# Own weights and reciprocals through a scratch in device memory, the maxima's copy on VectorE, and the reciprocals' rows behind the second stack pair

## The chip, the cores and the metric

The kernel runs on one core of a Trainium2 chip. The metric is the device time of that core in microseconds (us), from launch to end. Engines: TensorE (PE, its weight loads PEld), VectorE (DVE), ScalarE (ACT), GpSimd (POOL) and SyncE (SP), which here only issues DMAs. Each engine runs its own instructions in order and waits on semaphores that the others and the DMAs raise.

## The reference

Eight batches of 512 rows of width 512. A layer of cross attention with 16 heads of width 32 is added to x, and then a two-layer network of hidden width 2048, whose last 128 output columns come from one of eight experts per batch. Each query also attends to itself by one extra score, the "own" score.

```python
query = seq2 + b_self
key = jnp.concatenate([seq1 + b_prev, seq2 + b_self], 1)
value = jnp.concatenate([seq1, seq2], 1)
q, k, v = ...                                   # 16 heads of 32
score_prev = jnp.einsum('bhqd,bhkd->bhqk', q, k[:, :, :l1]) * SCALE
score_self = (q * k[:, :, l1:]).sum(-1, keepdims=True) * SCALE
score_prev = jnp.where(mask[:, None, None, :], score_prev, -jnp.inf)
weights = jax.nn.softmax(jnp.concatenate([score_prev, score_self], -1), axis=-1)
attn = jnp.einsum('bhqk,bhkd->bhqd', weights[..., :-1], v[:, :, :l1])
attn = attn + weights[..., -1:] * v[:, :, l1:]
x = x + (attn.transpose(0, 2, 1, 3).reshape(b, l2, H * DH) @ Wo + bo)
h = jax.nn.gelu(x @ W1 + b1, approximate=False)
x = x + jnp.concatenate([h @ W2 + b2, h @ We[indices] + be[indices]], axis=-1)
```

## The kernel before

**Stages.** First the attention of all eight batches (to about 1220 us of the span), then the output projection and the network, batch by batch. Matmuls are split into high and low parts, three matmuls per product. In attention a batch is four *groups* g of four heads each; group number G = 4 b + g. A group is 16 *tiles* i (four key blocks t times four heads j). The batches 1 to 6 are one hardware loop on every engine, batch 0 and batch 7 are unrolled. The order on each engine is written out by hand, by tables of places (g, i).

**A group on PE** (`batch` in the tensor block): per tile i one score matmul of group G (`score_tile`), the maximum matmuls of group G + 1 (`max_tile`), and thirds of the projections of group G + 2; in g = 0 also the value projections. At i = 11 come the denominators of group G - 1 (`denominators`), the own scores of G + 1 and the transpose of its maxima (`own_scores`, `turn_max`). After the last tile `value_run` multiplies the probabilities by the values.

**Around it.** ACT makes the probabilities p_f from the scores (`probabilities`), POOL adds them to p_sum (`add_probabilities`), DVE reduces the maximum tiles to m_col (`maximum`). The maximum matmuls of G + 1 read *stacks*, which SP copies from `parts` by DMA in two pairs of heads (`stack_pair(..., 0)` and `(..., 1)`, three DMAs per head, and a mask row in g = 2 and 3). The second pair may only be written once score tiles 14 and 15 of the present group have run. `m_col` holds four maxima per query block; `maxima_twice` doubles them to eight columns on ACT at i = 12, then `turn_max` turns them. DVE then takes the maximum with the own scores (`own_max`), splits it (`m_parts`) and SP and ACT copy it into the stacks (`maxima`). ACT turns the own scores into own weights in `own_s` (`own_weight`, i = 15).

**The two spreads.** `own_s` and `den` are 128 x 128 tiles in SBUF: row 32 t + j belongs to query block t and head j, and only 4 rows of each 32 mean anything. POOL needs the own weights (`own_value`) and DVE the reciprocals of the denominators (`normalize`) with each head's row repeated on 32 partitions: `own_rows` and `over_den_rows`, the two halves of the tile `spread`. SP makes each by four DMAs, one per query block t, whose source is four partitions, each read 32 times:

```python
def rows_of(tile, t):
    return bass.AP(tile[:, :].tensor, DH * t * P, [[P, HG], [0, DH], [1, P]])
```

**SP's order in a group**: in g = 0 and 1 the 16 input loads of the next batch (`load`, 64 KB each), which DVE turns at (0, 9) to (1, 15) (`turn`); the first stack pair of G + 2; `maxima` of G + 1; the reciprocals' rows of G - 1 (`over_den`); the second stack pair of G + 2; the own weights of G + 1 (`own_weights`); the store of the numerators of G - 2 (`store`). In batch 7 weight pieces for the second stage take the place of the loads (`wide`, `wide_late`), with `attended` and `residual` for its first batch.

## Time and profile before

| | us |
|---|---|
| median of 3 runs (2031.56 to 2033.59) | 2032.14 |
| the profiled execution | 2025.96 |
| its span, first to last instruction | 2024.1 |
| PE busy | 1760.7 (87%) |
| DVE, ACT, POOL busy | 839.9, 705.0, 651.8 |
| mean granted TensorE clock | 0.925 |
| shares of the chain that ended last: PE, SP's queue, DMAs, DVE, ACT | 72%, 18%, 5%, 2%, 1% |

The profiled execution took 1.9 us more than its span, and 6.2 us less than the median of the runs. Busy shares are means over two unlike stages: in the second one PE is busy all the time. So the page is read by stretches, a group of the attention at a time. A group ends where `value_run` (L1435) ends. Line numbers are those of the kernel before; a "hole" is time in which PE sits idle, and the row says what ended it.

### The profile page before, as it was taken

The numbers are of one execution on the slowest core, as the hardware profiler recorded it, in microseconds if no ns is written. First come the engines' busy times: TensorE is split into PE (matmuls) and PEld (weight loads), VectorE is DVE, ScalarE is ACT, GpSimd is POOL, SyncE is SP. The second block draws the span as 40 slices with busy tenths as digits, with TensorE's granted clock in tenths as the row PEclk, the third lists the DMA queues.
The fourth block names the chain that finished last, engine by engine and source line by source line (L and its number), as shares of the span: only waits on it lengthen the run. The fifth ranks groups of instructions, "written<-read, shape, count | busy, mean of one in ns | idle before, by whom it ended". The sixth has DMA issues, their size and how long they took to land.

```text
span 2024.1 us, 29434 instructions
## 1 busy us (share of the span) xinstructions
PE 1760.7 (87%) x9024; PEld 1335.4 (66%) x9024; DVE 839.9 (41%) x1338; ACT 705.0 (35%) x1255; POOL 651.8 (32%) x518
## 2 busy tenths in 40 slices
PE   6989879888788878788799546999999999999998
PEld 5656556556556556466566224888888888888886
DVE  4554454454544554454454623432323232323222
ACT  3344333334333433343344323432323232323231
POOL 2356356464563654645553422010101010101010
PEclk8989889989899889889799668999999999999999
DMA  6443443443534434444433343332313131413121
GB/s 136 75 82 71 86 85 78 78 86 75 94 81 77 87 70 91 80 82 75 85 75 74 95 88 104 107 61 68 74 51 78 47 78 47 83 44 81 46 42 21
DMA packets 379888, 153.69 MB, mean 76 GB/s; under 512 B 287571, under 2 KB 339795, under 8 KB 379811
## 3 DMA queue, kind: packets, MB, share of 16 engines
q1 hardware_dynamic: 374966, 152.05, 36.4%
q10 hardware_dynamic: 4844, 0.78, 0.2%
q8 instruction: 28, 0.46, 0.1%
q14 instruction: 50, 0.40, 0.1%
HBM read 60.97 MB, written 24.15 MB: 42 GB/s over the span
## 4 chain that ended last, share of the span: by engine, by line
PE 72%; SPq 18%; DMA 5%; issue 3%; DVE 2%; ACT 1%; DVEq 0%; POOL 0%; ACTq 0%
PE ps_proj L1354 14%; PE ps_max L1306 6%; PE ps_max L1308 6%; PE ps_max L1307 6%; SPq L390 5%; PE ps_score L1422 5%; PE ps_num L1435 5%; SPq L409 5%; PE ps_max L1395 4%; SPq L373 4%; PE ps_num L1306 3%; PE ps_num L1308 3%; PE ps_num L1307 3%; PE ps_score L1306 3%; PE ps_score L1308 3%; PE ps_score L1307 3%
## 5 line engine op out<-in xcount | busy, mean ns | idle before, releaser
L1016 DVE TENSOR_REDUCE m_col<-ps_max 128x1 f32<-128x512 f32 x512 | 335.5, 686 | 398.7 <-PE ps_max L1395 396.5
L794 ACT ACTIVATE p_f<-ps_score 128x512 f32<-128x512 f32 x512 | 302.6, 598 | 443.2 <-PE ps_score L1422 389.2
L670 POOL TENSOR_TENSOR p_sum<-p_sum,p_f 128x512 f32<-128x512 f32 x256 | 326.1, 1305 | 0.2 <-ACT p_f L794 0.2
L1395 PE MATMUL ps_max<-stacks 97*128 97x512 f32 x512 | 197.8, 438 | 86.9 <-DMA stacks<-parts 80.8
L1354 PE MATMUL ps_proj<-in_hi,w_hi 128*128 128x512 f32 x512 | 223.1, 436 | 48.3 <-DVE parts L998 36.0
L1209 DVE TENSOR_TENSOR h_lo<-h_f,h_hi 128x512 fp32r<-128x512 f32 x128 | 88.0, 688 | 414.2 <-ACT h_hi L898 414.0
L1422 PE MATMUL ps_score<-stacks 99*128 99x512 f32 x512 | 229.6, 450 | 29.5 <-ACT p_f L794 28.0
L712 POOL TENSOR_TENSOR z_f<-z_f,a_raw 128x512 f32<-128x512 f32 x28 | 35.8, 1290 | 676.9 <-ACT z_f L907 654.4
L1354 PE MATMUL ps_proj<-in_lo,w_hi 128*128 128x512 f32 x512 | 221.3, 432 | 0.0
L1354 PE MATMUL ps_proj<-in_hi,w_lo 128*128 128x512 f32 x512 | 217.7, 425 | 0.0
L667 POOL TENSOR_TENSOR p_sum<-p_f 128x512 f32<-128x512 f32 x128 | 168.0, 1334 | 71.3 <-PE ps_max L1449 71.3
L1395 PEld LDWEIGHTS ps_max<-stacks 97*128 97x128 f32 x512 | 105.4, 210 | 120.3 <-issue 78.6
L658 POOL TENSOR_TENSOR v<-v,spread 128x512 f32<-128x512 f32 x32 | 41.5, 1298 | 411.4 <-DMA spread<-own_s 411.4
L1422 PEld LDWEIGHTS ps_score<-stacks 99*128 99x128 f32 x512 | 106.2, 208 | 97.9 <-ACT p_f L794 41.9
L1354 PEld LDWEIGHTS ps_proj<-in_hi,w_hi 128*128 128x128 f32 x512 | 109.2, 213 | 77.3 <-DVE parts L998 39.6
L1354 PEld LDWEIGHTS ps_proj<-in_lo,w_hi 128*128 128x128 f32 x512 | 109.9, 215 | 26.6
L1354 PEld LDWEIGHTS ps_proj<-in_hi,w_lo 128*128 128x128 f32 x512 | 106.9, 209 | 26.1
L1435 PE MATMUL ps_num<-p_f,v_st 128*32 128x512 f32 x1024 | 118.4, 603 | 4.5 <-DVE num L1047 4.2
L675 POOL TENSOR_TENSOR in_lo<-turned,in_hi 128x512 fp32r<-128x512 f32 x64 | 80.9, 1291 | 115.5 <-ACT in_hi L732 115.4
L1306 PE MATMUL ps_num<-y_hi,w_hi 128*128 128x512 f32 x256 | 101.7, 397 | 16.7 <-ACT h_hi L898 9.4
L1307 PE MATMUL ps_num<-y_lo,w_hi 128*128 128x512 f32 x256 | 101.3, 396 | 0.0
L1308 PE MATMUL ps_num<-y_hi,w_lo 128*128 128x512 f32 x256 | 101.3, 396 | 0.0
(141 smaller groups left out, 2987.5 us busy)
## 6 DMA issues: line engine op xcount, KB each, us to landing
stacks<-parts SPq DMA_DIRECT2D x384, 128.0 KB, 2.4
raw<-in_x_dram SPq DMA_DIRECT2D x128, 64.0 KB, 2.1
raw<-in_fside_BxSxS_dram SPq DMA_DIRECT2D x128, 64.0 KB, 2.2
spread<-own_s SPq DMA_DIRECT2D x128, 64.0 KB
spread<-den SPq DMA_DIRECT2D x128, 64.0 KB
attn_scratch<-num SPq DMA_DIRECT2D x32, 256.0 KB, 7.2
x_raw<-in_x_dram SPq DMA_DIRECT2D x128, 64.0 KB, 2.1
we_raw<-in_L_cond_We_dram SPq DMA_DIRECT2D x32, 256.0 KB, 2.9
```

The costliest lines, as they stand in the source:

```text
L390: sp.dma_start(f(stacks[DH * part:DH * (part + 1), r, j]), f(pair)).then_inc(stacked[r][j], DMA)
L667: pool.tensor_tensor(p_sum[:, j], p_f[:, place_of(0, j)], p_f[:, i], ALU.add).then_inc(sum_made, 1)
L670: pool.tensor_tensor(p_sum[:, j], p_sum[:, j], p_f[:, i], ALU.add).then_inc(sum_made, 1)
L794: act.activation(p_f[:, i], ps_score[i % 2][:, :], ACT.Exp, scale=SCALE).then_inc(p_made, 1)
L1016: dve.tensor_reduce(m_col[:, n % C, n // C:n // C + 1], ps_max[n % 3][:, :], AX.X, ALU.max).then_inc(max_made, 1)
L1306: pe.matmul(ps, left[0], right[0], start=first, stop=False)
L1307: pe.matmul(ps, left[0], right[1], start=False, stop=False)
L1308: return pe.matmul(ps, left[1], right[0], start=False, stop=last)
L1354: mm = pe.matmul(ps, left, right, start=(m == 0), stop=(m == 3 * C - 1))
L1395: pe.matmul(ps_max[n % 3][:, :], q_st[0:KM, r, j, P * t:P * (t + 1)], k_st[0:KM, r, j, :], start=True, stop=True).then_inc(max_mm, 1)
L1422: pe.matmul(ps_score[i % 2][:, :], k_st[0:KS, r, j, P * t:P * (t + 1)], q_st[0:KS, r, j, :], start=True, stop=True).then_inc(score_mm, 1)
L1435: mm = pe.matmul(ps_num[at, :], v_st[:, t, P * g + DH * j:P * g + DH * (j + 1)], p_f[:, i], start=(t == 0), stop=(t == C - 1))
```

## The change

Own weights: ACT waits for its own activation and stores the whole tile `own_s` to a scratch in device memory (`own_scratch`), right after the activation at i = 15; SP then reads it back by four DMAs, one per head j, each from four rows of 512 bytes (one per query block) repeated over 32 partitions. Reciprocals: the same through `den_scratch`; ACT stores `den` after the last probabilities tile of the group, and for the very last group SP does. `over_den` stands behind the second stack pair instead of ahead of it, and at the end of attention behind `w2_piece(3)`. The doubling of the maxima on ACT (16 columns) is gone; DVE copies them to 28 more columns at i = 10 (`maxima_rows`), and `turn_max` and `denominators` make 32 rows per block instead of 8, so that all 128 rows of the tiles are defined. `m_hi` is gone: both steps of `m_parts` write `m_neg`, and the wait for the previous maxima's DMAs stands ahead of the first.

```diff
-            def rows_of(tile, t):
-
-                return bass.AP(tile[:, :].tensor, DH * t * P, [[P, HG], [0, DH], [1, P]])
-
             def own_weights(b, c):
 
                 G = C * b + c
-                sp.wait_ge(ow_made, G + 1)
-                for t in range(C):
-                    sp.dma_start(own_rows[:, P * t:P * (t + 1)], rows_of(own_s[c % 2], t)).then_inc(ow_landed, DMA)
+                sp.wait_ge(ow_stored, DMA * (G + 1))
+                for j in range(HG):
+                    sp.dma_start(own_rows[DH * j:DH * (j + 1), :].rearrange("k (t q) -> k t q", t=C),
+                                 own_dram[c % 2, :, j].partition_broadcast(DH)).then_inc(ow_landed, DMA)
...
             def over_den(b, c):
 
-                G = C * b + c
-                sp.wait_ge(rden_made, G + 1)
-                for t in range(C):
-                    sp.dma_start(over_den_rows[:, P * t:P * (t + 1)], rows_of(den, t)).then_inc(over_den_landed, DMA)
+                sp.wait_ge(den_stored, DMA * (C * b + c + 1))
+                for j in range(HG):
+                    sp.dma_start(over_den_rows[DH * j:DH * (j + 1), :].rearrange("k (t q) -> k t q", t=C),
+                                 den_dram[:, j].partition_broadcast(DH)).then_inc(over_den_landed, DMA)
...
-                    if more:
-                        stack_pair(*after(b, g, 2), 1)
...
+            store_over_den()
+            w2_piece(3)
             over_den(B - 1, C - 1)
-            w2_piece(3)
...
-            def maxima_twice(b, c):
-
-                G = C * b + c
-                act.wait_ge(max_made, TILES * (G + 1))
-                act.copy(m_col[:, :, HG:2 * HG], m_col[:, :, 0:HG]).then_inc(m_twice, 1)
-
...
                 act.activation(own_s[c % 2][:, :], own_s[c % 2][:, :], ACT.Exp, scale=SCALE).then_inc(ow_made, 1)
+                wait(act, ow_landed, HG * DMA * (G - 1))
+                act.wait_ge(ow_made, G + 1)
+                act.dma_start(own_dram[c % 2].rearrange("t k q -> (t k) q"), own_s[c % 2][:, :]).then_inc(ow_stored, DMA)
+
+            def store_over_den(b, c):
+
+                G = C * b + c
+                act.wait_ge(rden_made, G + 1)
+                wait(act, over_den_landed, HG * DMA * G)
+                act.dma_start(den_dram.rearrange("t k q -> (t k) q"), den[:, :]).then_inc(den_stored, DMA)
...
+            def maxima_rows(b, c):
+
+                G = C * b + c
+                dve.wait_ge(max_made, TILES * (G + 1))
+                dve.tensor_copy(m_col[:, :, HG:DH].rearrange("p t (n j) -> p t n j", j=HG),
+                                m_col[:, :, 0:HG].unsqueeze(2).to_broadcast([P, C, DH // HG - 1, HG])).then_inc(m_rows, 1)
...
-                dve.tensor_scalar(m_hi[:, :], m_s, -1.0, None, ALU.mult).then_inc(m_hi_made, 1)
                 pb, pc = after(b, c, -1)
                 wait(dve, m_landed[pc % 2], C * DMA * (2 * pb + pc // 2 + 1))
+                dve.tensor_scalar(m_neg[:, :], m_s, -1.0, None, ALU.mult).then_inc(m_hi_made, 1)
...
-                    mm = pe.matmul(ps_max[0][DH * t:DH * t + 2 * HG, 0:P], m_col[:, t, :], f(ident[:, :]),
+                    mm = pe.matmul(ps_max[0][DH * t:DH * (t + 1), 0:P], m_col[:, t, :], f(ident[:, :]),
...
-                    one_at = ones[:, C - 1 - j:C - 1 - j + 2 * HG]
+                    one_at = ones[:, HG - 1 - j:HG - 1 - j + DH]
```

SP, group (0, 2) from its `maxima` to its `store`, before. `spread<-den` are the reciprocals' rows, `spread<-own_s` the own weights', `stacks<-parts` here the second stack pair with its mask row:

```order
L397 DMA stacks<-m_neg 2x4x128 [waits m_lo_made]
L397 DMA stacks<-m_neg 2x4x128
L416 DMA spread<-den 128x1x128 [waits rden_made]
L416 DMA spread<-den 128x1x128 x3
L384 DMA stacks<-mask_scratch 1x2x512 [waits score_mm]
L390 DMA stacks<-parts 32x1024 [waits score_mm]
L390 DMA stacks<-parts 32x2x512 x2
L409 DMA spread<-own_s 128x1x128 [waits ow_made]
L409 DMA spread<-own_s 128x1x128 x3
L420 DMA attn_scratch<-num 128x512 [waits attn_made]
```

The same place now:

```order
L399 DMA stacks<-m_neg 2x4x128 [waits m_lo_made]
L399 DMA stacks<-m_neg 2x4x128
L386 DMA stacks<-mask_scratch 1x2x512 [waits score_mm]
L392 DMA stacks<-parts 32x1024 [waits score_mm]
L392 DMA stacks<-parts 32x2x512 x2
L420 DMA spread<-den_scratch 32x4x128 [waits den_stored]
L420 DMA spread<-den_scratch 32x4x128 x3
L407 DMA spread<-own_scratch 32x4x128 [waits ow_stored]
L407 DMA spread<-own_scratch 32x4x128 x3
L425 DMA attn_scratch<-num 128x512 [waits attn_made]
```

The stack pair moved ahead of both spreads, these now stand side by side, their shape went from 128 x 1 x 128 to 32 x 4 x 128, and they wait for a DMA's landing instead of an engine.

ACT, group (0, 1) from i = 12 to its end, before:

```order
L766 COPY m_col<-m_col 128x4x4 [waits max_made]
L773 COPY own_s<-ps_max 128x128 [waits den_made,ow_landed,own_mm]
L794 ACTIVATE p_f<-ps_score 128x512 [waits sum_made,av_mm,score_mm] x2
L780 DMA stacks<-m_neg 2x4x128 [waits m_lo_made]
L780 DMA stacks<-m_neg 2x4x128
L794 ACTIVATE p_f<-ps_score 128x512 [waits sum_made,av_mm,score_mm]
L787 ACTIVATE own_s<-own_s 128x128 [waits ov_made,own_less_made]
L794 ACTIVATE p_f<-ps_score 128x512 [waits sum_made,av_mm,score_mm]
L732 CAST in_hi<-turned 128x512 [waits v2_mm,turn_made] x4
```

and now:

```order
L773 COPY own_s<-ps_max 128x128 [waits den_made,ow_stored,own_mm]
L804 ACTIVATE p_f<-ps_score 128x512 [waits sum_made,av_mm,score_mm] x2
L780 DMA stacks<-m_neg 2x4x128 [waits m_lo_made]
L780 DMA stacks<-m_neg 2x4x128
L804 ACTIVATE p_f<-ps_score 128x512 [waits sum_made,av_mm,score_mm]
L787 ACTIVATE own_s<-own_s 128x128 [waits ov_made,own_less_made]
L790 DMA own_scratch<-own_s 128x128 [waits ow_made,ow_landed]
L804 ACTIVATE p_f<-ps_score 128x512 [waits sum_made,av_mm,score_mm]
L797 DMA den_scratch<-den 128x128 [waits rden_made]
L738 CAST in_hi<-turned 128x512 [waits v2_mm,turn_made] x4
```

The copy of the maxima left ACT, and a store now stands on each side of the last probabilities tile.

## Rows read from the trace of the kernel before

**Rows 1.** Windows (length; busy of PE, PEld, DVE, ACT, POOL; PEclk, DMA share, GB/s).

```profile
812.00:848.70 36.70, 27.48 (x161) 18.75 (x161) 18.87 (x31) 15.96 (x31) 21.07 (x17) 0.86 0.49 92
848.70:881.60 32.90, 26.85 (x165) 18.95 (x162) 15.84 (x27) 12.00 (x23) 19.73 (x17) 0.90 0.38 74
881.60:913.20 31.60, 27.32 (x161) 18.82 (x162) 16.18 (x27) 12.00 (x23) 17.44 (x15) 0.89 0.38 76
...
194.10:1055.30 861.20, 711.15 (x4133) 503.23 (x4129) 420.79 (x696) 325.27 (x624) 457.22 (x361) 0.90 0.43 81
...
1090.70:1220.00 129.30, 75.61 (x401) 44.51 (x400) 57.32 (x80) 42.21 (x81) 52.65 (x41) 0.72 0.39 85
...
1055.30:1090.70 35.40, 35.35 (x213) 26.09 (x209) 16.27 (x27) 14.16 (x27) 19.27 (x16) 1.00 0.35 69
...
595.00:623.00 28.00, 24.07 (x160) 16.66 (x158) 15.84 (x27) 12.03 (x23) 13.29 (x12) 1.00 0.41 83
...
102.90:194.10 91.20, 79.81 (x485) 56.12 (x481) 49.65 (x84) 40.41 (x77) 49.50 (x40) 0.91 0.43 81
```

**Rows 2.** Waits, whole span (engine, line, releaser: total us, times, longest).

```profile
PE ps_max L1395 <- DMA stacks<-parts: 80.8, 21, 6.0
...
DVE turned L990 <- DMA raw<-in_fside_BxSxS_dram: 49.3, 10, 7.8
...
PE ps_max L1412 <- ACT m_col L766: 48.0, 9, 7.2
...
PE ps_proj L1354 <- DVE parts L998: 36.0, 6, 7.5
```

**Rows 3.** Timeline of SP's queue, 806 to 846 (start, length, line, DMA, count).

```profile
807.73 5.85 SPq L416 DMA_DIRECT2D spread<-den  x4
813.70 7.98 SPq L390 DMA_DIRECT2D stacks<-parts  x6
821.72 6.11 SPq L409 DMA_DIRECT2D spread<-own_s  x4
828.12 2.24 SPq L420 DMA_DIRECT2D attn_scratch<-num  x1
830.54 10.67 SPq L373 DMA_DIRECT2D raw<-in_fside_BxSxS_dram  x16
841.49 3.96 SPq L390 DMA_DIRECT2D stacks<-parts  x6
```

**Rows 4.** Windows, as rows 1: spreads alone, then stacks behind loads.

```profile
783.00:787.00 4.00, 4.00 (x19) 3.25 (x18) 1.17 (x2) 1.67 (x3) 0.00 (x0) 1.00 0.18 23
...
843.00:845.00 2.00, 2.00 (x10) 1.44 (x8) 2.00 (x4) 1.02 (x2) 0.00 (x0) 1.00 0.88 197
```

**Rows 5.** Page part 6: DMA issues, KB each, median us to landing.

```profile
stacks<-parts SPq DMA_DIRECT2D x384, 128.0 KB, 2.4
raw<-in_x_dram SPq DMA_DIRECT2D x128, 64.0 KB, 2.1
...
resid_scratch<-a_raw SPq DMA_DIRECT2D x28, 256.0 KB, 2.0
```

**Rows 6.** Timeline of all engines, end of a group, from 900.

```profile
907.81 1.27 ACTq L780 DMA_DIRECT2D stacks<-m_neg  x2
...
909.51 3.64 PE L1435 MATMUL ps_num<-p_f,v_st 128*32 128x512 f32 x32
```

**Rows 7.** Lines by form (count | busy us, mean ns | idle before).

```profile
L1449 PEld LDWEIGHTS ps_max<-p_sum,ones 128*8 128x8 f32 x992 | 24.4, 91 | 12.8 <-issue 8.0 <-DVE m_col L1016 4.4
...
L1067 DVE TENSOR_TENSOR wo_lo<-raw,wo_hi 128x512 fp32r<-128x512 f32 x4 | 8.3, 2067 | 0.1
L1404 PEld LDWEIGHTS ps_max<-qk_f,sum_heads 128*32 128x32 f32 x256 | 7.7, 112 | 0.8 <-issue 0.7
```

**Rows 8.** Waits from 1090 to 1262, as rows 2.

```profile
PE ps_score L1422 <- ACT p_f L794: 26.1, 11, 12.4
...
PE ps_num L1306 <- ACT h_hi L898: 9.4, 1, 9.4
```

More of the change, by code:

```diff
@@ L199, in cond_resid_program @@
         m_landed = [sem(f"m_landed{r}") for r in range(2)]
-        m_twice = sem("m_twice")
+        m_rows = sem("m_rows")
         own_less_made, ow_made = sem("own_less_made"), sem("ow_made")
-        ow_landed = sem("ow_landed")
+        ow_stored, ow_landed = sem("ow_stored"), sem("ow_landed")
+        den_stored = sem("den_stored")
         over_den_landed = sem("over_den_landed")
@@ L506, in batch @@
                         residual(0, 3)
+                    if more:
+                        stack_pair(*after(b, g, 2), 1)
                     if not (first and g == 0):
                         over_den(*after(b, g, -1))
-                    if more:
-                        stack_pair(*after(b, g, 2), 1)
                     if last and g == 2:
@@ L685, in _ @@
             pool.wait_ge(den_ones_made, 1)
-            pool.memset(ones[:, C - 1:C], 1.0).then_inc(den_ones_made, 1)
+            pool.memset(ones[:, HG - 1:DH + HG - 1:HG], 1.0).then_inc(den_ones_made, 1)
             def batch(b, first, last):
@@ L770, in own_row @@
                 act.wait_ge(own_mm, G + 1)
-                wait(act, ow_landed, HG * DMA * (G - 1))
+                wait(act, ow_stored, DMA * (G - 1))
                 wait(act, den_made, G - 1)
@@ L825, in _ @@
             v2_out(0, 1)
-            maxima_twice(0, 0)
             own_row(0, 0)
@@ L847, in batch @@
                             maxima(*nxt, range(2, C))
+                        if i == 15 and not (first and g == 0):
+                            store_over_den(*after(b, g, -1))
                         if i == 0 and maximum and not (first and g == 0):
@@ L966, in _ @@
                 rows = slice(DH * j, DH * (j + 1))
-                dve.memset(sum_heads[rows, j:2 * HG:HG], 1.0).then_inc(zeros_made, 1)
+                dve.memset(sum_heads[rows, j:DH:HG], 1.0).then_inc(zeros_made, 1)
             dve.wait_ge(consts_made, 3)
@@ L1029, in m_parts @@
                 dve.wait_ge(m_s_made, G + 1)
[L1030 removed]
                 pb, pc = after(b, c, -1)
                 wait(dve, m_landed[pc % 2], C * DMA * (2 * pb + pc // 2 + 1))
+                dve.tensor_scalar(m_neg[:, :], m_s, -1.0, None, ALU.mult).then_inc(m_hi_made, 1)
                 dve.wait_ge(m_hi_made, G + 1)
[L1034 removed]
+                dve.scalar_tensor_tensor(out=m_neg[:, :], in0=f(m_neg[:, :]), scalar=less_hi[:, 0:1], in1=m_s,
                                          op0=ALU.mult, op1=ALU.subtract).then_inc(m_lo_made, 1)
@@ L1053, in denominator @@
                 dve.wait_ge(den_mm, G + 1)
-                wait(dve, over_den_landed, HG * DMA * G)
+                wait(dve, den_stored, DMA * G)
                 dve.tensor_tensor(den[:, :], ps, own_s[g % 2][:, :], ALU.add).then_inc(den_made, 1)
@@ L1123, in _ @@
                     q_low(0, 1)
+            maxima_rows(0, 0)
             qk(0, 1)
@@ L1138, in batch @@
                                 maximum(*nxt, n)
+                        if i == 10 and bound:
+                            maxima_rows(*nxt)
                         if not last:
```

17 lines of the change are left out of this document (10 added, 7 removed).

## Prediction, made before the changed kernel was run

> **What bounds the kernel now.** I read the chain that ended last first: 72% of it lies on PE, but 18% on SP's queue and 5% on DMAs (the table of the profile), so issuing transfers sets part of the time. The windows by group say where. In batches 1 to 6 the attention takes 861.2 us, 143.5 a batch, at a granted clock of 0.90 [rows 1]. Two stretches show what a group costs when nothing is late: group (7, 0), which has no input loads, took 35.4 us with PE busy 35.35 at clock 1.00, and in 28 us of (3, 3), all 160 matmuls of the group, PE was busy 24.07 at clock 1.00 [rows 1]. With small gaps a group with g over 0 needs 24.5. A batch without holes is 35.4 + 3 x 24.5 = 108.9 us, so 34.6 us a batch are holes and the lower clock after them (the clock was 0.86 to 0.90 in the groups shown).
>
> The waits name the holes: PE waits for stacks to land (80.8 us, 21 times), for ACT's copy of the maxima (48.0, 9 times, at most 7.2), and for DVE's low part of k (36.0, 6 times) [rows 2]. The second looks like ACT's fault, but DVE was itself waiting for input loads (49.3 us, 10 times, at most 7.8 [rows 2]), in g = 1 with the turn that stands ahead of its last maxima. In g = 0 the low part of k stands behind such a turn too. So all three are late transfers on SP's queue.
>
> That queue in g = 1 of batch 5: 5.85 us for four reciprocals' reads, 7.98 for the second stack pair, 6.11 for four own reads, 2.24 for the store, 10.67 for 16 loads, 3.96 for the next six stack copies [rows 3]. That is 36.8 us, and the group took 36.7 [rows 1]: SP is full. Six stack copies cost 3.96 us (0.66 each) away from a spread and 7.98 behind one; so the spreads also cost the two transfers behind each of them some 2 us apiece. While only spreads were moving, the DMA engines were busy 0.18 at 23 GB/s; with stacks and loads 0.88 at 197 GB/s [rows 4]. 0.18 of 16 is about three engines, and a 64 KB spread at 23 GB/s takes 2.8 us, more than SP needs to issue it: the queue backs up.
>
> **The spreads by head.** The new reads have 32 rows on both sides. The Trainium skill, page "DMA: Bandwidth & Descriptors", section "Why a DMA increments its semaphore by 16 and not by 1", says a DMA runs on the largest number of engines up to 16 that divides the slowest dimension of source and destination: 4 of (4, 128) before, 16 of (32, 32) now. The 0.18 agrees with the first; the second would cut a read from 2.8 to about 0.7 us.
>
> No row shows a repeated read from device memory. Its bounds: below, 0.53 us, the pitch of a 64 KB load in a run (in [rows 3] 16 loads in 10.67, of which the first, backed up, took some 2.7, hence 15 in 8.0); above, the present 2.8. The nearest row by shape is the stack copy, also 32 partitions wide: 0.66. I take 0.66, so four reads cost 2.6.
>
> SP in g = 1 then: second pair 4.0, two spreads 5.3, store 0.6, loads 8.5, first pair 4.0, two copies of maxima 1.3: 23.7 us against 24.5 a group. It fits, barely, and in g = 0 (35.4) and in g = 2 and 3 (no loads) with room.
>
> **The order and the new waits.** The second pair may start when score tiles 14 and 15 have run, and now does; it lands (2.4 us [rows 5]) about 2 us into the next group, which wants it at its i = 5, about 7 us in. That hole ends, also at the dearest read. ACT's wait for its own activation and the store come between the activation and the last p_f tile. An ACT issue costs 0.64 (1.27 for two [rows 6]); with some 0.3 of wait that tile comes 1.0 later, while `value_run`, 3.64 us long [rows 6], needs it only in its last quarter: covered by some 1.5. Without that cover it would cost 32 x 1.0. The second store comes after the tile, again 0.64, before the next group's first score. Behind it in g = 1 stand four casts for POOL, which has until the middle of g = 2. A store of 256 KB lands in 2.0 us without backlog [rows 5]; so `den` is in memory about 0.5 us into the next group, just as SP has finished the pair, and SP reaches the loads at about 6.5. The first set of four loads is in SBUF at 6.5 + 4 x 0.53 + 2.1 = 10.7 [rows 5]; its turn stands at i = 9, at about 12 (tiles of (24.5 - 3.6) / 16 = 1.3 us). Queued behind SP's new wait are the own reads, the store, the loads and the first pair; the last has maxima behind it, which leave at 20.3 and are wanted at 24.5. Slack 1 to 2 us at each place.
>
> ACT loses its copy of maxima, DVE gains one of 112 columns (0.2 to 0.4 us, in a group where it is busy 18.9 of what would be 24.5 [rows 1]); it stands behind the last maximum, while PE still has four projection matmuls, the denominators and the own scores ahead of `turn_max`: nothing. The moved wait in `m_parts` is for DMAs a group old: nothing. Loads of weights go from 8 to 32 columns, 91 to 112 ns [rows 7]: at most 40 x 0.02 = 0.8 a group, if loads bound those; denominators overlap them, and I take 0.1, 3 us in all, bounds 0 to 26.
>
> **The sum**, against the profiled 2026. Not everything will arrive in time: I leave 2 us a batch in g = 1, where SP has no slack, and 1.3 elsewhere, so 112.2 a batch and 31.3 gained.
> - Batches 1 to 6: 6 x 31.3 = 188, bounds 57 (below) and 208.
> - Batch 0, groups 1 to 3: 91.2 [rows 1] to 3 x 25.1 = 75: 16.
> - Batch 7, groups 1 to 3: 129.3 us with PE busy 75.6 [rows 1]; the holes for p_f alone are 26.1 [rows 8], where ACT waits for weight pieces that stand behind six spreads. Each spread of four gives back 3.3 on itself and some 4 on the transfers behind it, but `over_den` now waits for ACT's last tile, 2 to 3 us. I take 25, bounds 8 and 45.
> - End of attention: the hole of 9.4 for h_hi [rows 8] is ACT waiting for `w2_piece(3)`, which stood behind four spreads and now stands ahead: 7, bounds 0 and 14.
> - PE's wider loads: -3.
>
> Together 188 + 16 + 25 + 7 - 3 = 233: 1793 for a profiled run, and 6 more for the median of runs: **1799**.
>
> **Rivals.** *The reads from memory stay slow* (A). All 32 copies of a head come from the same 2 KB. If that place delivers no more than now, a read stays at 2.5 to 2.8. Then the second pair's move alone pays: about 8 us in g = 2, 6 in g = 3, 3 in g = 1, less 7 because eight spreads in a row now back up together ahead of the loads of g = 0 and 1. That is some 9.5 a batch, 57, and 12 for batches 0 and 7: 1963. Against it stands the 197 GB/s of other transfers [rows 4]. By the Trainium skill, page "SBUF — State Buffer", section "A bandwidth-pool intuition that's wrong (but worth ruling out)", memory is reached through 32 ports of about 22.5 GB/s, so one port would need 2.9 us for 64 KB, an estimate from that page; no row shows a read bound so.
>
> *The same, dearer* (B, slower). The loads of g = 0 and 1 stand behind eight such reads, 12 groups: each further us on a read costs 96. The 69 of rival A are gone at 2.5 + 0.7 = 3.2 us a read, and over 3.3 the kernel is slower by more than 0.2%; at 4 us it is 2032 - 69 + 144 = 2107.
>
> *Another engine becomes late* (C). POOL's additions run end to end from the denominators on, and DVE's subtraction of two SBUF tiles beside them took 2.07 us on the mean of four [rows 7]. With POOL busy 76 us a batch (457 by six [rows 1]) of what would be 112, one such wait of 3 to 5 us in each of two or three groups outlasts the slack: 10 a batch, 1860.
>
> **How the numbers follow.** Forecast 0.75, C 0.10, A 0.10, B 0.03, and 0.02 that nothing moves beyond noise, because the gained time turns into a new wait. The forecast's own range is 1755 (nearly all holes gone) to 1840. The range for 8 in 10 takes it and C in, and leaves out A, B and the tails: 1755 to 1900. Faster by over 0.2% (what a measurement can tell here): forecast, C and A, 0.95; within 0.2%, 0.02; slower, 0.03.
>
> **What would show it.** SP's timeline: reads at 0.6 to 0.7 in the queue, the transfers behind them too (right), or 2.4 from the third on (A). No wait of PE for stacks, with L1412's counterpart and the low part of k under 3 us a batch. Groups of 35 and 25 us, clock 0.97 or more. If SP idles in g = 1 while PE has holes named by POOL or DVE, it is C. I am wrong if stores or reads land over 4 us after issue, or if ACT's last p_f tile is what `value_run` waits for.

## The result, and the profile after

| | before | after |
|---|---|---|
| median of runs, us | 2032.87 (2031.56 to 2035.87) | 1754.99 (1753.96 to 1756.97) |
| ratio, 95% interval | | 0.8632 [0.8617, 0.8647] |
| the profiled execution, its span | 2025.96, 2024.1 | 1755.05, 1752.9 |
| PE busy | 1760.7 (87%) | 1687.3 (96%) |
| mean granted clock | 0.925 | 0.982 |

The change takes 277.9 us. The forecast was 1799, with a range from 1755 to 1900: the direction and most of the mechanism held, the size did not, and the median lies just under the low end.

I read the chain that ended last first (part 4 of the page), by engine:

```profile
PE 86%; DVE 5%; issue 4%; SPq 2%; DMA 2%; ACT 0%; DVEq 0%; ACTq 0%; POOL 0%
```

SP's queue fell from 18% to 2%, and PE holds 86%. The windows say where the time went (length; busy of PE, PEld, DVE, ACT, POOL; clock, DMA share, GB/s): batches 1 to 6; groups 1 to 3 of batch 0; groups (5, 0) and (5, 1); groups 1 to 3 of batch 7, then (7, 2) and (7, 3) alone.

```profile
171.60:829.40 657.80, 648.76 (x4129) 466.25 (x4129) 432.82 (x720) 323.76 (x600) 464.54 (x361) 1.00 0.50 111
98.10:171.60 73.50, 72.48 (x483) 51.44 (x481) 53.45 (x87) 39.83 (x74) 52.87 (x42) 1.00 0.47 105
610.20:646.30 36.10, 35.37 (x209) 26.23 (x209) 19.23 (x32) 14.15 (x26) 17.42 (x14) 1.00 0.49 105
646.30:670.50 24.20, 24.10 (x162) 17.16 (x161) 18.60 (x32) 15.99 (x30) 20.48 (x17) 1.00 0.70 146
864.80:958.20 93.40, 72.86 (x404) 43.96 (x400) 54.34 (x82) 42.22 (x78) 53.46 (x41) 0.80 0.47 114
889.20:918.10 28.90, 22.66 (x113) 10.86 (x113) 23.05 (x34) 14.50 (x28) 20.15 (x15) 0.70 0.36 101
918.10:958.20 40.10, 26.04 (x128) 15.89 (x128) 14.54 (x20) 15.81 (x28) 17.14 (x14) 0.74 0.53 113
```

Beside [rows 1]: batches 1 to 6 went from 861.2 to 657.8 us, 109.6 a batch, with PE idle for 9 of 658 us at clock 1.00. Group (5, 1) went from 36.7 to 24.2. Batch 7 is where holes are left, 20.5 of 93.4 us, and the clock there is 0.80.

| stretch | before | after | gained | forecast |
|---|---|---|---|---|
| group (0, 0) | 102.9 | 98.1 | 4.8 | none |
| batch 0, groups 1 to 3 | 91.2 | 73.5 | 17.7 | 16 |
| batches 1 to 6 | 861.2 | 657.8 | 203.4 | 188 |
| group (7, 0) | 35.4 | 35.4 | 0 | 0 |
| batch 7, groups 1 to 3 | 129.3 | 93.4 | 35.9 | 25 |
| the rest | 804.2 | 794.7 | 9.5 | 7 |
| wider weight loads | | | in the above | -3 |

Of the 203.4 us, 141.0 are idle time of PE in these six batches (150.0 before, 9.0 now), and 62.4 are PE's own busy time, which shrank from 711.2 to 648.8 for the same matmuls as the granted clock rose from 0.90 to 1.00.

The waits of PE, whole span, some of the rows (engine, line, releaser: us in total, times, longest):

```profile
PE ps_score L1442 <- ACT p_f L804: 8.6, 9, 4.8
...
PE ps_proj L1326 <- DVE a_lo L1089: 6.3, 1, 6.3
...
PE ps_proj L1374 <- DVE parts L1008: 3.9, 6, 0.6
...
PE ps_max L1432 <- DVE m_col L1033: 1.9, 3, 1.0
```

The wait for stacks (80.8 us, [rows 2]) is gone; that for the maxima's copy went from 48.0 to 1.9, and that for the low part of k from 36.0 to 3.9. SP's queue in the group that answers to [rows 3] (start, length, line, DMA, count):

```profile
646.34 1.81 SPq L420 DMA_DIRECT2D spread<-den_scratch  x4
648.27 1.79 SPq L407 DMA_DIRECT2D spread<-own_scratch  x4
650.34 0.38 SPq L425 DMA_DIRECT2D attn_scratch<-num  x1
650.89 8.60 SPq L375 DMA_DIRECT2D raw<-in_fside_BxSxS_dram  x16
660.89 3.85 SPq L392 DMA_DIRECT2D stacks<-parts  x6
664.78 1.38 SPq L399 DMA_DIRECT2D stacks<-m_neg  x2
666.28 3.92 SPq L392 DMA_DIRECT2D stacks<-parts  x6
```

Eight reads take 3.6 us of the queue where they took 12.0, the store 0.38 us where it took 2.24, the 16 loads 8.60 where they took 10.67, and the pair that stood behind a spread 3.92 where it took 7.98. The seven rows add up to 21.7 us, in a group of 24.2. So in this group the reads themselves gave back 8.4 us and what stood behind them 8.0: both halves of the argument from [rows 3] are there.

### The profile page after: what moved, and what is told of

The parts are those of the page before. It is cut to its first block, busy times and chain, and to the rows that moved or that the text cites. A ratio compares the mean times of both kernels' runs of the same rounds, so it can differ in the third digit from the quotient of the medians.

```text
span 1752.9 us, 29583 instructions
## 1 busy us (share of the span) xinstructions
PE 1687.3 (96%) x9024; PEld 1291.2 (74%) x9024; DVE 855.9 (49%) x1370; ACT 702.6 (40%) x1223; POOL 661.6 (38%) x518
## 3 DMA queue, kind: packets, MB, share of 16 engines
q1 hardware_dynamic: 378182, 152.13, 38.3%
q10 hardware_dynamic: 13916, 4.91, 1.1%
## 4 chain that ended last, share of the span: by engine, by line
PE 86%; DVE 5%; issue 4%; SPq 2%; DMA 2%; ACT 0%; DVEq 0%; ACTq 0%; POOL 0%
PE ps_proj L1374 17%; PE ps_max L1415 7%; PE ps_max L1327 6%; PE ps_max L1326 6%; PE ps_max L1328 6%; PE ps_num L1455 6%; PE ps_score L1442 6%; PE ps_proj L1396 5%; PE ps_num L1326 3%; PE ps_num L1327 3%; PE ps_num L1328 3%; PE ps_score L1326 3%; PE ps_score L1327 3%; PE ps_score L1328 3%; PE ps_max L1469 2%
## 5 line engine op out<-in xcount | busy, mean ns | idle before, releaser
L1442 PE MATMUL ps_score<-stacks 99*128 99x512 f32 x512 | 213.6, 419 | 8.6 <-ACT p_f L804 8.6
L1374 PE MATMUL ps_proj<-in_hi,w_hi 128*128 128x512 f32 x512 | 205.6, 402 | 13.9 <-POOL in_lo L681 6.7
L1374 PE MATMUL ps_proj<-in_lo,w_hi 128*128 128x512 f32 x512 | 204.0, 399 | 0.0
L1374 PE MATMUL ps_proj<-in_hi,w_lo 128*128 128x512 f32 x512 | 204.0, 398 | 0.0
L1415 PE MATMUL ps_max<-stacks 97*128 97x512 f32 x512 | 182.9, 405 | 4.5 <-DVE m_col L1026 3.7
L1374 PEld LDWEIGHTS ps_proj<-in_hi,w_hi 128*128 128x128 f32 x512 | 98.2, 192 | 39.3 <-DVE parts L1008 7.4
L1415 PEld LDWEIGHTS ps_max<-stacks 97*128 97x128 f32 x512 | 98.3, 192 | 31.4 <-DVE m_col L1026 8.9
L1374 PEld LDWEIGHTS ps_proj<-in_lo,w_hi 128*128 128x128 f32 x512 | 98.4, 192 | 22.7
L906 ACT ACTIVATE h_f<-ps_num,bias 128x512 f32<-128x512 f32 x64 | 44.0, 687 | 161.1 <-PE ps_num L1328 127.0
L1326 PE MATMUL ps_score<-h_hi,w_hi 128*128 128x512 f32 x256 | 99.9, 390 | 1.9 <-DVE h_lo L1229 1.6
L1326 PE MATMUL ps_max<-y_hi,w_hi 128*128 128x512 f32 x256 | 99.9, 390 | 1.5 <-ACT h_hi L908 1.5
```

The costliest lines, as they stand in the source:

```text
L1326: pe.matmul(ps, left[0], right[0], start=first, stop=False)
L1374: mm = pe.matmul(ps, left, right, start=(m == 0), stop=(m == 3 * C - 1))
L1415: pe.matmul(ps_max[n % 3][:, :], q_st[0:KM, r, j, P * t:P * (t + 1)], k_st[0:KM, r, j, :], start=True, stop=True).then_inc(max_mm, 1)
L1442: pe.matmul(ps_score[i % 2][:, :], k_st[0:KS, r, j, P * t:P * (t + 1)], q_st[0:KS, r, j, :], start=True, stop=True).then_inc(score_mm, 1)
```

## Experiments

Three things were open. Which part of the change carries the gain: the reads, the order or the copy. Why the old reads were slow: the prediction said four engines instead of sixteen (theory E); the rival says that reading the same small strip of SBUF is slow in itself (theory P). And where the 44 us between forecast and result are. The kernel before, measured again beside the runs below, had medians from 2030.97 to 2032.83 us, so a difference of 2 or 3 us between two versions says little by itself.

### One part alone

**The order alone**, on the kernel before:

```diff
-                    if not (first and g == 0):
-                        over_den(*after(b, g, -1))
                     if more:
                         stack_pair(*after(b, g, 2), 1)
+                    if not (first and g == 0):
+                        over_den(*after(b, g, -1))
```

> The kernel before with one edit alone: the second stack pair is issued ahead of the reciprocals' reads. All reads still come from SBUF in the old four-row form. Theory S (the old reads back the queue up, the order is a small part): the holes for stacks in groups 2 and 3 go, the reads now stand eight in a row ahead of the loads of groups 0 and 1; about 1965 us as rival A of the prediction had it (57 less in batches 1 to 6, 12 in batches 0 and 7), and SP's queue in group (5, 1) stays full: 36 us of issues in a group of 35. Rival O (the order is what gained): 1750 to 1800, SP with idle time in every group. A loss (over 2032) would say that eight old reads in a row hurt the loads by more than the pair gains.

Measured: 1980.0 us, ratio 0.9749 [0.9726, 0.9773]. That is 52 us, a fifth of the gain. Batches 1 to 6 took 822.7 us, 38.5 less than before; the forecast of rival A had 57. The waits of PE between 102.5 and 1013 us:

```profile
PE ps_max L1412 <- ACT m_col L766: 61.6, 7, 11.3
PE ps_num L1435 <- DVE num L1047: 48.9, 13, 5.2
PE ps_proj L1354 <- DVE parts L998: 20.9, 6, 4.0
```

The stacks' wait is gone as a whole, and 48.9 us came in its place: value products that wait for DVE's `num`. DVE in turn waited as many times for the store of the numerators, two groups older, to land:

```profile
DVE num L1047 <- DMA attn_scratch<-num: 54.5, 13, 5.8
```

SP's queue, from (5, 1) on, shows why that store is late:

```profile
785.32 9.61 SPq L409 DMA_DIRECT2D spread<-own_s  x4
795.22 1.76 SPq L420 DMA_DIRECT2D attn_scratch<-num  x1
797.16 10.44 SPq L373 DMA_DIRECT2D raw<-in_fside_BxSxS_dram  x16
807.88 3.94 SPq L390 DMA_DIRECT2D stacks<-parts  x6
```

Eight old reads in a row stand ahead of the store: the second four now take 9.61 us instead of 6.11, while the pair, free of them, takes some 3.9 for 7.98. The store and the 16 loads cost no more than before (1.76 and 10.44 us). By group, the mean gain in batches 1 to 6 was 2.5 us in g = 0, 1.4 in g = 1, 1.9 in g = 2 and 0.6 in g = 3: in g = 2 and 3, where the stacks' holes had been, the waits for `num` stand now, 2.1 to 5.2 us each.

**The copy alone**, on the kernel before (its 16 columns by DVE behind the last maximum):

```diff
-                            maxima_twice(*nxt)
                             own_row(*nxt)
...
+                        if i == 10 and bound:
+                            maxima_twice(*nxt)
```

> The kernel before with one edit alone: the doubling of the 16 maxima columns is done by DVE behind its last maximum instead of by ACT; everything else as before. The waits of before put 48.0 us on ACT's copy in nine places. Theory S: ACT's copy was late since DVE's maxima stood behind a turn that waited for loads, so the hole only changes its name to DVE: 2025 to 2033, nothing beyond noise. Rival M (ACT's queue made it late): up to 48 less, 1985.

Measured: 2031.5 us, ratio 0.9998 [0.9986, 1.001]. The wait of 48.0 on ACT's copy in [rows 2] turned into this one:

```profile
PE ps_max L1413 <- DVE m_col L1015: 43.6, 9, 7.6
```

Nine times again, with DVE's name: ACT's queue was not what made it late.

**The copy back to ACT**, on the kernel after:

> The kernel after, with the copy that fills the maxima's other 28 columns done by ACT ahead of own_row (where before had its copy of 16 columns) instead of by DVE. The prediction costed the move to DVE at nothing. Theory (nothing: four projection products, the denominators and the own scores stand ahead of turn_max on PE): 1753 to 1757. Rival (ACT reaches the copy a tile or more later, up to 1.3 us after DVE would): some 1 us in each of 31 groups, 1785, PE waiting for ACT's m_col at its weight load.

Measured: 1754.6 us (1751.71 to 1756.85), beside 1754.99. Batches 1 to 6 took 657.8 us in both. The move to DVE is worth nothing that can be measured.

**The order of before in the kernel after** (the two lines of the first diff the other way round):

> The kernel after with the order of before alone: the reciprocals' reads stand ahead of the second stack pair again. The pair then waits for ACT's store of den to land (it did by 696.9 us or sooner in the group that ends at 695.5) and for 2.0 us of reads, so it would leave at about 699 to 703.6 instead of 692.3 to 696.9 and land at about 706, where PE wants it some 7 us into the group, at 702.5. Theory S: holes of 1 to 3 us a group in 31 groups, 1785 to 1850, best guess 1810, still far below before: the reads' new form carries most of the gain. Rival O: over 1900. Rival N (SP now has so much slack that the order is worth nothing): 1753 to 1760.

Measured: 1761.31 us, 6 more than after. My best guess of 1810 was wrong, and rival N was nearly right. The pair leaves at 700.8 to 704.7 in a group that began at 698.7:

```profile
698.14 1.75 SPq L420 DMA_DIRECT2D spread<-den_scratch  x4
700.07 0.64 SPq L386 DMA_DIRECT2D stacks<-mask_scratch  x1
700.83 3.84 SPq L392 DMA_DIRECT2D stacks<-parts  x6
```

The last of its six copies does land at 706.5, as expected, but the first head of the pair needs three of them, and these had landed at 704.5. PE's first maximum product on it ran at 705.7, with no hole in front. I had taken the pair for one thing that is late when its last copy is. So with quick reads the order is worth at most 6 us: batches 1 to 6 took 661.1 us for 657.8, and part of the rest is group (7, 2), of which more below. With slow ones it is worth 52.

### Why the old reads were slow

**The old cut, from memory**: the kernel after, its reads by block t as before, of four rows of 512 bytes, each for 32 partitions.

```diff
-                for j in range(HG):
-                    sp.dma_start(own_rows[DH * j:DH * (j + 1), :].rearrange("k (t q) -> k t q", t=C),
-                                 own_dram[c % 2, :, j].partition_broadcast(DH)).then_inc(ow_landed, DMA)
+                for t in range(C):
+                    sp.dma_start(own_rows[:, P * t:P * (t + 1)], rows_in_memory(own_dram[c % 2, t, 0:HG])).then_inc(ow_landed, DMA)
```

> The kernel after, but the eight reads a group are cut as before: by block t, four rows of memory 512 B each repeated for 32 partitions, 64 KB each, source now device memory. Only the cut of the reads differs from after, only the place of the source from before's reads. Theory E (four rows on the slow side put a DMA on four engines): reads cost about 2.4 to 2.8 us each from the third on as before, and the kernel goes back to some 1900 to 2000, since only the order of the pair is left of the gain. Theory P (it was the place in SBUF, one small strip read over and over, that was slow; memory isn't): reads at 0.43 to 0.6 in the queue, 1753 to 1765.

Measured: 1757.36 us, ratio to before 0.8651 [0.8632, 0.867]; batches 1 to 6 took 657.7 us. Theory E, on which the prediction built its price, falls as the cause of the slow reads: with the same cut into four rows, four reads cost 2.32 and 2.18 us of the queue:

```profile
671.47 2.32 SPq L422 DMA_DIRECT2D spread<-den_scratch  x4
673.92 2.18 SPq L410 DMA_DIRECT2D spread<-own_scratch  x4
```

**Half the change**: the kernel after, its own reads alone taken from SBUF in the old form.

```diff
-                for j in range(HG):
-                    sp.dma_start(own_rows[DH * j:DH * (j + 1), :].rearrange("k (t q) -> k t q", t=C),
-                                 own_dram[c % 2, :, j].partition_broadcast(DH)).then_inc(ow_landed, DMA)
+                for t in range(C):
+                    sp.dma_start(own_rows[:, P * t:P * (t + 1)], rows_of(own_s[c % 2], t)).then_inc(ow_landed, DMA)
```

> The kernel after, with its own-weight reads alone taken from SBUF in the old four-row form again (ACT's store to memory stays, so only the source and cut of four reads a group differ from the run by block). Theory P: these four back the queue up as before: two at 0.6, two at 2.4, and the store and first load behind them 1 to 2.4 each, about 8 us more on SP, of which g = 1 has 1.4 free and g = 0, 2, 3 about 8: 6 to 7 us of hole a batch and some clock, 1790 to 1830. Rival L (slow reads hurt only when eight stand together, four are absorbed): 1755 to 1765. Rival H (half of the gain hangs on each spread): about 1890.

Measured: 1824.01 us, ratio to before 0.8969 [0.8951, 0.8987]: 69 us above after. The own reads have the shape that they had in the run by block; what differs for them is the source. SP's queue in (5, 1):

```profile
689.07 6.73 SPq L410 DMA_DIRECT2D spread<-own_s  x4
696.09 2.40 SPq L427 DMA_DIRECT2D attn_scratch<-num  x1
698.68 11.29 SPq L375 DMA_DIRECT2D raw<-in_fside_BxSxS_dram  x16
```

The old reads cost 6.73, and the store and loads behind them 4.7 more than in after. Only g = 1 pays in batches 1 to 6 (31.4 us on the mean for 24.2; g = 0 has 36.1 in both). DVE waits there for the loads, and PE for DVE:

```profile
DVE turned L1003 <- DMA raw<-in_fside_BxSxS_dram: 37.1, 7, 5.9
...
PE ps_max L1435 <- DVE m_col L1036: 37.4, 7, 6.2
```

This is the chain of names that the prediction read out of [rows 2], now made on purpose.

**The forms by themselves**: a probe behind the end of the kernel.

> The kernel after, and behind its last instruction a probe on SP's queue alone, with nothing else running: five forms of the repeated read, each a burst of four DMAs of 64 KB, then twice a burst of eight, each burst waited for (the one-row form: 16, 32 and 32 DMAs of 16 KB). The output is untouched. The forms: (1) four rows of SBUF side by side, each repeated 32 times, as before had them; (2) the same, but the four rows 20 partitions apart; (3) four rows of device memory side by side, as in the run by block; (4) 32 repeats of four 512 B rows of memory, by head, as after has them; (5) one row of SBUF, 32 repeats, 16 KB. Theory P (a small strip of SBUF read over and over is slow in itself): form 1 takes 2.4 us or more a DMA in a burst of eight, 3 and 4 take 0.43 to 0.6. Then form 2 tells whether it is the neighbourhood of the rows (it falls to a quarter, 0.6 to 0.9) or the number of rows, or SBUF as a source (it stays at 2.4). Form 5: if one row of SBUF is what delivers so little, 16 KB take 0.6 to 2.4 us each in a long burst. Theory E (four rows on the slow side mean few engines) is out by the run by block unless form 3, alone on the queue, is slow as well.

Measured in one execution, the first burst of eight (32 in the last form) of each; the timeline of SP's queue:

```profile
1764.70 16.22 SPq L679 DMA_DIRECT2D a_raw<-x_t  x8
...
1812.31 4.78 SPq L679 DMA_DIRECT2D a_raw<-x_t  x8
...
1833.10 4.36 SPq L679 DMA_DIRECT2D a_raw<-own_scratch  x8
...
1853.50 3.62 SPq L679 DMA_DIRECT2D a_raw<-own_scratch  x8
...
1877.92 20.52 SPq L679 DMA_DIRECT2D a_raw<-x_t  x32
```

and the windows of the same bursts (no engine works, so only the last two columns count: DMA share and GB/s):

```profile
1766.00:1780.00 14.00, 0.00 (x0) 0.00 (x0) 0.00 (x0) 0.00 (x0) 0.00 (x0) 0.50 0.18 26
1812.00:1819.00 7.00, 0.00 (x0) 0.00 (x0) 0.00 (x0) 0.00 (x0) 0.00 (x0) 0.50 0.23 68
1833.00:1840.00 7.00, 0.00 (x0) 0.00 (x0) 0.00 (x0) 0.00 (x0) 0.00 (x0) 0.50 0.23 69
1853.50:1859.00 5.50, 0.00 (x0) 0.00 (x0) 0.00 (x0) 0.00 (x0) 0.00 (x0) 0.50 0.37 93
1878.00:1898.00 20.00, 0.00 (x0) 0.00 (x0) 0.00 (x0) 0.00 (x0) 0.00 (x0) 0.50 0.19 25
```

A burst of eight, until all had landed and the next could start, less the burst of four, over four, is what one more DMA costs: form 1, (21.05 - 12.74) / 4 = 2.1 us; form 2, (7.94 - 4.78) / 4 = 0.8; form 3, (8.03 - 4.91) / 4 = 0.8; form 4, (6.19 - 4.33) / 4 = 0.5. For form 5 it is (22.09 - 11.72) / 16 = 0.65 for 16 KB, 2.6 for 64 KB; since its issues stand 0.64 apart, the queue alone could set that.

So the cut matters, but little: forms 2 and 3, four rows on the slow side at a share of 0.23 of 16, cost 0.8, and form 4, by head at 0.37, cost 0.5. The large factor is where the four rows lie in SBUF. Side by side they give 26 GB/s at a share of 0.18, 20 partitions apart 68 GB/s at 0.23, and one row alone 25 GB/s. Both shares are near the 0.25 that four busy engines of 16 would show; that in form 1 these four wait for the strip is my reading, not something a view shows. Nor were rows tried that lie more than 1 and fewer than 9 partitions apart, or four neighbours that don't start at a multiple of four. So it is open whether distance as such counts or a fixed group of four. The share of 0.18 in [rows 4], on which the prediction rested its price, could not tell the two apart.

The Trainium skill, page "SBUF — State Buffer", section "Door 1: The DMA port swizzle (why `[64,N]` ≈ `[32,N]`)", says that four neighbouring partitions from a multiple of four on lie behind one of 16 ports for DMAs, and that partitions 0 to 3 gave 27.6 GB/s. The 26 GB/s here agrees, with the reserve that a burst took four such strips in turn (32 rows apart) and no run read from one alone. 64 KB at 27.6 GB/s would be 2.4 us, an estimate from that page; 2.1 was measured. The prediction had cited another section of it, on the ports of device memory at 22.5 GB/s, with an estimate of 2.9 us a read. Here the reads from memory cost 0.8 and 0.5 us, again over four places in turn.

### Without device memory

If only the neighbourhood of the rows is at fault, the detour through memory isn't needed. In after each block of `own_s` and `den` holds every head in eight rows, row r being head r mod 4, so four heads can be read from rows 0, 9, 18 and 27. The kernel after without both stores, and with

```diff
+            def rows_of(tile, t):
+                return bass.AP(tile[:, :].tensor, DH * t * P, [[(2 * HG + 1) * P, HG], [0, DH], [1, P]])
...
-                sp.wait_ge(ow_stored, DMA * (G + 1))
-                for j in range(HG):
-                    sp.dma_start(own_rows[DH * j:DH * (j + 1), :].rearrange("k (t q) -> k t q", t=C),
-                                 own_dram[c % 2, :, j].partition_broadcast(DH)).then_inc(ow_landed, DMA)
+                sp.wait_ge(ow_made, G + 1)
+                for t in range(C):
+                    sp.dma_start(own_rows[:, P * t:P * (t + 1)], rows_of(own_s[c % 2], t)).then_inc(ow_landed, DMA)
```

> The kernel after without device memory in the path: both stores and both scratch tensors' use are gone, the reads come from SBUF by block t again, but take the four heads from rows 0, 9, 18 and 27 of the block instead of 0, 1, 2, 3. That is possible since in after every block holds each head in eight rows (row r is head r mod 4). Order as in after. The probe had 0.54 us a read in the queue for rows 20 apart and 2.1 to 2.8 for rows side by side. Theory P (neighbouring rows are the whole fault): reads at 0.54, no stack hole, no wait for a store: batches 1 to 6 as in after, batch 7 and batch 0 the same or a little shorter, 1745 to 1757. Rival (9 partitions are too near): reads over 1 us from the third on, 1850 to 1990.

Measured: 1749.66 us (1748.78 to 1752.12), ratio to before 0.8616 [0.86, 0.8632], 5 under after. Batches 1 to 6 took 657.7 us. The reads in the queue:

```profile
669.40 2.44 SPq L417 DMA_DIRECT2D spread<-den  x4
671.88 2.76 SPq L411 DMA_DIRECT2D spread<-own_s  x4
```

0.6 to 0.7 a read, a little more than from memory, but with no store ahead of it. What is gained lies mostly behind the attention: the rest of the span is 790.5 us for 794.7, and PE's hole behind the last `value_run` is 0.9 us for 3.6. So none of the 277.9 us needs memory: memory was one way off the strip of four neighbouring rows, and putting the rows apart is another.

### The slack, and the last batch

**Four times as many own reads**, of 16 KB:

```diff
                 for j in range(HG):
-                    sp.dma_start(own_rows[DH * j:DH * (j + 1), :].rearrange("k (t q) -> k t q", t=C),
-                                 own_dram[c % 2, :, j].partition_broadcast(DH)).then_inc(ow_landed, DMA)
+                    for t in range(C):
+                        sp.dma_start(own_rows[DH * j:DH * (j + 1), P * t:P * (t + 1)],
+                                     own_dram[c % 2, t, j].partition_broadcast(DH)).then_inc(ow_landed, DMA)
```

> The kernel after, with its four own-weight reads a group cut into sixteen of 16 KB (one block and head each): the same bytes, twelve more issues on SP. It tests how much room SP's queue has left. By the timeline of after, SP issues for about 22.8 of the 24.2 us in g = 1 (reads 3.6, store 0.4, 16 loads 8.6, stack copies 9.2, small gaps), so about 1.4 us are free there; g = 0, 2 and 3 have 8 or more. Theory (SP in g = 1 is still the next bound): 12 x 0.43 = 5.2 us more, 3.8 over the slack, 7 times, with a little clock: 1775 to 1800, best guess 1783, and PE waiting for maxima rows or stacks at the end of g = 1 alone. Rival (POOL's late reads: own_rows landing 5 us later delays POOL's product in every group): over 1800. If a small read costs 0.1 or less, nothing: 1755.

Measured: 1775.5 us (1773.69 to 1777.37), the low edge of the theory's range. The sixteen took 7.32 us of the queue, 5.5 more. Batches 1 to 6 lost 8.5 us (666.3), 1.4 on the mean of each g = 1 and nothing in the other groups; the rest of the loss is in batch 7 (5.0), group (0, 0) (3.4) and the end (1.8). So SP in g = 1 is the next bound, but it had some 4 us of slack (5.5 more issued, 1.4 lost) and not the 1.4 that the expectation took from its idle time. I put that down to transfers at the group's end that leave ahead of need; this wasn't tried apart. Of the 5.0 us in batch 7, 3.0 are in (7, 2), of which more below.

**ACT's store twice**, each behind its activation:

> The kernel after, with ACT issuing its store of the own weights twice (the second to another place in memory that nobody reads), between its activation and the last p_f tile of each group. The prediction held that value_run covers 1.5 us there. Theory: the second issue, 0.64 us, is covered in batches 0 to 6, so 1755 to 1758. Rival (no cover: ACT's added work sits on PE's path): 31 x 0.64 = 20, 1775, and PE waits for ACT's p_f before its last value products.

Measured: 1760.38 us (1757.34 to 1762.95). Batches 1 to 6 lost 1.2 us, where 24 uncovered issues would cost 15: the cover by `value_run` holds. The whole is still 2 us over the theory's 1758: group (7, 2) lost 3.5, and the next run shows in what.

**The weight pieces of (7, 2) first**:

```diff
+                    if last and g == 2:
+                        for n in range(9, EARLY):
+                            wide(n)
                     if not (first and g == 0):
                         over_den(*after(b, g, -1))
                     if last and g == 2:
-                        for n in range(9, EARLY):
-                            wide(n)
```

> The kernel after, with the three weight pieces of group (7, 2) issued ahead of over_den instead of behind it. In after SP stands at over_den from 911.9 to 916.2 us (it waits for ACT's store of den), so the pieces leave at 918.0 to 919.0 and land at 923.3 to 924.6; group (7, 3) has a hole of 4.8 us while ACT, behind its cast of the first of them, is late with p_f. Theory: they land at about 915 to 917 and that hole goes; 1749 to 1752. Rival (the hole then opens at the next input, attended or residual, which stay where they are): 1753 to 1756.

Measured: 1757.44 us (1755.85 to 1757.57), no gain. The pieces landed at 917.6 to 919.1, and the hole went from 4.8 to 2.8. But groups (7, 2) and (7, 3) took 69.5 us for 69.0, since a hole of 5.4 opened in (7, 2), where DVE's `wo_lo` stands ahead of a maximum (after, then this run):

```profile
891.27 0.83 DVE L1084 TENSOR_TENSOR wo_lo<-raw,wo_hi 128x512 fp32r<-128x512 f32 x1
```

```profile
890.90 5.73 DVE L1084 TENSOR_TENSOR wo_lo<-raw,wo_hi 128x512 fp32r<-128x512 f32 x1
891.15 4.93 POOL L676 TENSOR_TENSOR p_sum<-p_sum,p_f 128x512 f32<-128x512 f32 x4
```

The same instruction takes 0.8 us or 5.7, and in the second case it ends 0.6 us behind POOL's run of additions. Nothing that this edit moves comes ahead of 890 us, so that hole isn't its doing. The first `wo_lo` took 5.7 to 7.0 us in ten of the fourteen traces (6.24 in before, 6.96 with ACT's store twice), and 0.8 to 1.5 in after, in the run by block, and in those of the order and of the copy alone. Group (7, 2) took 28.9 us in after and 29.4 in the run by block; in the traces of the other quick versions it took 31.0 to 33.3. So after is a lucky one here by some 2 to 3 us, which is enough to hide what an edit in batch 7 brings.

**The rows 9 apart, with both orders of batch 7**: the edit above, and

```diff
+                        attended(0, 3)
                         wide_late(EARLY)
                         wide_late(EARLY + 1)
                         wide_late(EARLY + 2)
-                        attended(0, 3)
```

> The kernel of the rows 9 apart, and beside it the order of the last batch changed: the three weight pieces of (7, 2) ahead of over_den, and attended(0, 3) ahead of the three pieces of (7, 3). In after attended(0, 3) left at 929.8 and landed at 936.4, and PE waits 6.3 us behind its low part. Theory: it lands 2 to 4 us sooner, and with the hole of 4.8 us gone the last two groups lose 6 to 9 of their 20 us of idle time: 1742 to 1750. Rival (another input is last there at once, ACT's casts in order): 1750 to 1757.

Measured: 1745.68 us (1745.2 to 1746.16), ratio to before 0.8592 [0.8577, 0.8607]: the best version here, 9 under after. Against the rows 9 apart alone, (7, 2) took 31.6 us in both, and (7, 3) 33.3 for 36.7; the waits of PE in batch 7, rows 9 apart, then both orders:

```profile
PE ps_proj L1309 <- DVE a_lo L1072: 7.1, 1, 7.1
PE ps_max L1398 <- DVE m_col L1009: 5.9, 2, 5.4
PE ps_score L1425 <- ACT p_f L789: 5.0, 9, 1.9
```

```profile
PE ps_max L1398 <- DVE m_col L1009: 5.9, 2, 5.4
PE ps_score L1425 <- ACT p_f L789: 5.4, 9, 2.6
PE ps_proj L1309 <- DVE a_lo L1072: 3.0, 1, 3.0
```

`attended(0, 3)` landed at 931.1 us for 934.5, and the wait behind it is 4.1 shorter, which covers the gain; the waits for p_f did not get shorter, so the pieces' order seems to have brought nothing here either. The two edits were not run apart on this kernel.

## Why the prediction was right, and where it was wrong

**Right: what bounds.** SP's queue was the bound, three holes with three names came from it, and the transfers behind a spread paid as much as the spread. The runs show each: the copy alone moves nothing, half the change brings 69 us back through loads and DVE, and in after the reads gave 8.4 us a group and what stood behind them 8.0.

**Right: what costs nothing.** DVE's copy (1754.6 with it on ACT), and ACT's stores and the waits for them to land in batches 1 to 6 (657.7 us with no store at all). Behind the attention they did cost some 4 us, as the rows 9 apart show. Rival B did not come. Rival C, a DVE subtraction that loses against POOL's additions, came only in (7, 2), and there it was no news: the mean of 2.07 us in [rows 7] is one `wo_lo` of 6.24 and three of 0.68.

**Near in number, wrong in reason: the price of a read.** It took 0.66 us; 0.45 to 0.5 was measured. The reason, four engines against sixteen, explains at most 0.8 against 0.5, not 2.1; that the price came out near was luck. Had the change kept the cut by block, the prediction would have forecast little gain and been wrong by some 200 us. Rival A named the same 2 KB strip as a danger for memory; it was the fault of SBUF before.

**Right sign, too high: the order alone.** Rival A's 69 us for the order with slow reads measured 52. Its gains of 8 us in g = 2 and 6 in g = 3 failed: 1.9 and 0.6 were measured, since eight reads in a row hold up the store that DVE's `num` waits for, 48.9 us of waits in all, a path that it did not have. The loss of 7 through the loads of g = 0 and 1, against a gain of 3 there, did not come: these two groups gained 3.9 together.

**Wrong: the sum, by 44 us**, in these terms.
- Batches 1 to 6: 188 forecast, 203.4 measured, 15.4 short. The step that failed is "not everything will arrive in time": 3.3 us a batch were kept in hand on top of a floor of 108.9, and 0.7 was needed. SP in g = 1 issues for 21.7 us and not 23.7, nearly all of it by the price of a read (3.6 us for eight instead of 5.3), and the run with sixteen reads found some 4 us of slack.
- Batch 7, groups 1 to 3: 25 forecast, 35.9 measured, 10.9 short, inside the bounds of 8 and 45. The waits for p_f fell from 26.1 us [rows 8] to 8.6; the term was set near the middle of its bounds without a row for it. Some 2 to 3 us of the gain may be the short `wo_lo` in (7, 2) of this trace.
- Group (0, 0): 4.8, not in the sum at all. It holds one spread of own weights. With own reads of the old form it took 102.5 to 104.5 us (before, the order alone, the copy alone, half the change), with quick ones 96.7 to 98.7 (101.5 with sixteen of them); within each kind it differs by 2, so some of the 4.8 may not be the change's.
- The end: 7 forecast, 9.5 measured. The wait of 9.4 for h_hi was 9.7 with the order alone, which leaves `w2_piece(3)` where it was, and 1.1 at most with half the change, which moves it. That fits the prediction's cause, but the piece alone wasn't tried.
- PE's wider loads: -3 forecast. They did go from 91 to 111 ns (992 loads each), and no group got longer: 0.
- Batch 0, groups 1 to 3: 16 forecast, 17.7 measured.
- The 6 us from profiled run to median: before's profiled run was 6.2 us under the median then known (6.9 under that of the result), after's 0.1 above. It was the luck of one run and not a term.

15.4 + 10.9 + 4.8 + 2.5 + 3 + 1.7 = 38.3, and 6 is 44.

**Wrong: the low end.** Its own bounds reached 208 + 16 + 45 + 14 = 283 without the wider loads, hence 2026 - 283 + 6 = 1749. It was set to 1755 as "nearly all holes gone" instead, and left no place for what the sum had not counted.

## What to carry to other kernels

- For a broadcast read inside SBUF look at where its rows lie: four neighbouring ones cost 2.1 us per 64 KB and back the queue up for whatever stands behind; four that lie 20 partitions apart cost 0.8, and 9 apart 0.6 to 0.7 of the queue. Other distances weren't tried. If a tile can hold its rows spread, or several times, take them apart before going through memory.
- A low DMA share does not say why so few bytes come: it was 0.18 at 26 GB/s and 0.23 at 68. Change the source or the cut alone before putting a price on it.
- Where a queue is full, add up what it would issue without the slow transfers. If that fits, count the holes as gone, and keep a reserve in the range, not in the sum; and let the range reach as far as the bounds of the terms do.

## What the runs showed of the hardware

- One DMA more of 64 KB, on a queue with nothing else (the probe), from four SBUF rows side by side: 2.1 us; 20 partitions apart: 0.8; four rows of memory: 0.8; by head, 32 repeats of four rows of memory: 0.5.
- The first two slow reads of a burst cost the queue 0.5 to 0.8 us each, like quick ones, the third and later ones 2.0 to 3.0 (form 1). A transfer of another kind behind them pays as well: the store behind four slow reads took 2.40 us with half the change, and 0.38 in after.
- The same VectorE operation on two SBUF tiles took 0.8 to 1.5 us in four traces and 5.7 to 7.0 in ten, beside GpSimd's additions of SBUF tiles. The Trainium skill, page "SBUF — State Buffer", section "SBUF: two separate sides", says that such an operation and one of GpSimd that reads SBUF exclude each other for a whole instruction. Here it stood through four additions (4.93 us), so it lost its turn more than once; why isn't shown by these runs.
